# One stream for all 16 pairs of expert and batch, and ScalarE normalising the first batch in the joint norms

## The chip, the cores and the metric

The kernel runs on one core of one Trainium2 chip. The metric is the device time of one execution in microseconds; several executions are made and their median is compared. A trace of one profiled execution gives the rows below.

## The reference, cut to what matters

Two layers, each a mixer followed by a feed-forward part, on x of 2 batches x 1024 tokens x 128 features, with a layer norm ahead of each of the four parts (A: gated linear scan and a SiLU network; B: six blocks of windowed attention and GELU network; C: linear attention; D: mixture of experts) and a norm with a residual addition behind each. The two pieces that the change touches:

```python
def norm(x):                       # layer norm; the rms form leaves the mean out
    return (x - mean(x)) / sqrt(var(x) + 1e-5)

# part D: 8 experts choose 128 tokens each, per batch
affinity = softmax(norm(x) @ gate_w)                  # [B, S, 8]
for b in range(2):
    for e in range(8):
        places = the 128 tokens of batch b with the highest affinity to e
        h = norm(x)[b, places]                        # gather, 128 x 128
        h = silu(h @ Wg[e]) * (h @ Wu[e]) * affinity[b, places, e]
        y[b, places] += h @ Wd[e]                     # scatter
x = x + norm(y)
```

## The kernel before

Tokens lie 128 to a tile, NT = 8 tiles a batch, B = 2 batches; S = 1024, HALF = 512 columns is one PSUM bank (PS is 8 banks). Features lie on the partitions in the feature-major layout. Each engine's program is written by hand in blocks; a block ends in a barrier of all engines. Within a block semaphores called flows order the engines: one engine's instruction increments a flow, another's waits for the next count.

`norm(*parts)` (L209) is called ten times in source; nine calls are joint, with one part for each batch, and the tenth, inside the loop of part D, has a single part and runs twice. Its VectorE program (L232) makes statistics of every part in halves of four tiles (bn_stats L239, bn_aggr L242, variance plus epsilon L253, in the rms form L247 and L250), then normalises every tile of every part in `normalise` (L255), one tile an instruction (L261 in the rms form, L265 otherwise), into NTOK, then adds the residual, if there is one, with one instruction a part (L278). GpSimd raises the variance to the power -0.5 for each half (L288). PE transposes normalised tiles (L226) where the part has a destination in feature-major layout, and ScalarE copies each half from PSUM to the destination (L298). A source in feature-major layout is transposed to tokens first (L218). Of the nine joint calls four have a token source and a destination (L330, L518, L1129, L1478), two are rms with a feature source and a destination (L331, L388), three have a feature source and a residual (L459, L1060, L1402). The final norm (L1750) reads tokens from PSUM and has a residual.

Part D: after the lists of places are made, a hardware loop runs over the batches (L1605). In it a block copies the normalised tokens and affinities to TOK (L1631 ScalarE, L1635 VectorE) and clears a zero tile, the next block runs the experts, and the norm follows. `step(n, i)` handles expert n and prepares expert n + 1 (n + 2 on VectorE); `run` executes steps -2 and -1, a hardware loop of three iterations of two steps, and the last two. In a step PE does in this order: gather of expert n + 1 with a one-hot matrix (L1645, 8 matmuls), transposes of the hidden tile HD of expert n (L1652), broadcast of the places of expert n + 1 to all partitions, two banks, each one matmul (L1660), transpose of the chosen tokens (L1665), down projection (L1670), gate and up projection of n + 1 (L1676), scatter with the transposed one-hot matrix into banks 6 and 7 (L1682, 8 matmuls). Ahead and behind, L1688 and L1692 open and close the accumulation of those banks with a zero product. A float32 matmul counts as two instructions in the trace, a transpose as one. ScalarE makes the sigmoid (L1701) and copies out of PSUM (L1705 chosen, L1709 hidden transposed HTD, L1712, L1716). VectorE multiplies (L1724, L1727), compares the broadcast places with its own partition's place for the transposed one-hot (L1733, 1024 columns), and makes the one-hot of expert n + 2 (L1740). There is one one-hot buffer and one transposed one.

## Time and profile before

| | |
|---|---|
| median of 3 runs | 2147.94 us (2147.43 to 2148.8) |
| the profiled execution, its time | 2145.2 us |
| its span | 2143.4 us |
| PE busy | 1921.5 us, 90% of the span |
| VectorE busy | 1709.2 us, 80% |
| ScalarE busy | 1400.0 us, 65% |
| GpSimd busy | 1245.5 us, 58% |
| chain that ended last | VectorE lines of the last norm, 0% each |
| stages on the trace's axis | A to 113.4, B to 1802, C to 1940, D to the end; part B's own program from 124 to 1785 |

In the rows below DVE is VectorE, ACT ScalarE, POOL GpSimd, PEld PE's weight load. A row of a timeline has the start, the time from the first start to the last end, the engine, the line, the operation, output and inputs, the shape and the count; in brackets stands the idle time of the engine before it and what ended it. The profile's names leave out numbers at the end: COSL in part D is the one-hot pair of buffers, QKT and XB the tokens, SQ the sigmoid, R and RR the hidden tiles.

### The profile page before, as it was taken

The numbers are of one execution on the slowest core, as the hardware profiler recorded it, in microseconds if no ns is written. First come the engines' busy times: TensorE is split into PE (matmuls) and PEld (weight loads), VectorE is DVE, ScalarE is ACT, GpSimd is POOL, SyncE is SP. The second block draws the span as 40 slices with busy tenths as digits, with TensorE's granted clock in tenths as the row PEclk, the third lists the DMA queues.
The fourth block names the chain that finished last, engine by engine and source line by source line (L and its number), as shares of the span: only waits on it lengthen the run. The fifth ranks groups of instructions, "written<-read, shape, count | busy, mean of one in ns | idle before, by whom it ended". The sixth has DMA issues, their size and how long they took to land. (4 is left out here: it accounts for less than half of the span.)

```text
span 2143.4 us, 79777 instructions
## 1 busy us (share of the span) xinstructions
PE 1921.5 (90%) x33524; PEld 1454.4 (68%) x33524; DVE 1709.2 (80%) x3962; ACT 1400.0 (65%) x5039; POOL 1245.5 (58%) x871
## 2 busy tenths in 40 slices
PE   4769999999999999999999999999999984491677
PEld 2348778687786886868868688687786862251455
DVE  5689889698796996979969789698896965787544
ACT  3159779597695985968959689597795961340222
POOL 2258768388584885857858668586683841031000
PEclk8879999999999999999999999999999997795799
DMA  3011112021120211212112121021110100001000
GB/s 113 0 42 42 31 50 58 21 78 35 44 59 22 76 39 36 58 29 73 41 35 57 33 69 44 24 63 40 51 52 17 42 26 13 0 2 60 1 1 20
DMA packets 88224, 85.65 MB, mean 40 GB/s; under 512 B 15392, under 2 KB 83008, under 8 KB 87232
## 3 DMA queue, kind: packets, MB, share of 16 engines
q1 hardware_dynamic: 87872, 80.63, 13.5%
q8 instruction: 260, 4.26, 0.8%
q14 instruction: 92, 0.75, 0.1%
HBM read 25.51 MB, written 1.05 MB: 12 GB/s over the span
## 5 line engine op out<-in xcount | busy, mean ns | idle before, releaser
L1050 POOL TENSOR_TENSOR RN<-N,minus_half 128x8 f32<-128x8 f32 x384 | 632.5, 1647 | 169.3 <-DVE N L978 169.3
L888 ACT ACTIVATE PB<-PS,NMX 128x64 f32<-128x64 f32 x1536 | 469.5, 334 | 30.3 <-DVE NMX L998 30.2
L647 PE MATMUL PS<-WQ,XS 128*128 128x256 f32 x1536 | 434.6, 406 | 7.5 <-SPq L591 5.9
L888 ACT ACTIVATION_READ_ACCUMULATOR PB<-PS,NMX 128x1 f32 x1536 | 344.7, 224 | 0.0
L647 PEld LDWEIGHTS PS<-WQ,XS 128*128 128x128 f32 x1536 | 261.3, 190 | 44.5 <-SPq L591 6.1
L1045 POOL TENSOR_TENSOR RR<-R 128x512 f32<-128x512 f32 x192 | 244.4, 1273 | 78.1 <-DVE QK L1008 78.1
L871 ACT ACTIVATE QKT<-PS 128x512 f32<-128x512 f32 x384 | 229.0, 596 | 87.3 <-PE PS L733 87.2
L1045 POOL TENSOR_TENSOR RR<-R1B,R2B 128x512 f32<-128x512 f32 x192 | 245.0, 1276 | 69.4 <-DVE QK L1008 69.4
L1008 DVE SCALAR_TENSOR_TENSOR QK<-RN,RR 128x512 f32<-128x512 f32 x384 | 261.7, 681 | 0.6 <-POOL RR L1045 0.6
L978 DVE TENSOR_REDUCE N<-SQ 128x8 f32<-128x512 f32 x384 | 259.5, 676 | 0.0
L854 ACT ACTIVATE SQ<-PS 128x512 f32<-128x512 f32 x384 | 237.1, 617 | 8.0 <-PE PS L647 7.7
L754 PE MATMUL PS<-WQ,XS 128*128 128x128 f32 x1536 | 234.2, 275 | 0.0
L733 PE MATMUL PS<-ident,QK 128*128 128x128 f32 x1536 | 230.8, 273 | 2.4 <-DVE QK L1008 2.1
L879 ACT ACTIVATE XB<-PS 128x512 f32<-128x512 f32 (+1 forms) x386 | 232.8, 603 | 0.1
L288 POOL TENSOR_TENSOR rstd<-ve,minus_half 128x4 f32<-128x4 f32 x40 | 40.4, 1010 | 320.0 <-DVE ve L253 292.1
L733 PEld LDWEIGHTS PS<-ident,QK 128*128 128x128 f32 x1536 | 191.7, 141 | 47.2 <-issue 6.2
L794 PE MATMUL PS<-XB,VS 64*64 64x32 f32 x6144 | 212.1, 224 | 2.0 <-ACT BIG L860 1.8
L794 PE MATMUL PS<-XB 64*64 64x32 f32 x6144 | 204.4, 219 | 1.1 <-issue 1.1
L754 PEld LDWEIGHTS PS<-WQ,XS 128*128 128x128 f32 x1536 | 201.7, 192 | 0.0
L794 PEld LDWEIGHTS PS<-XB,VS 64*64 64x64 f32 x6144 | 162.0, 133 | 37.3 <-ACT BIG L860 1.8
L998 DVE TENSOR_REDUCE NMX<-PS 128x4 f32<-128x256 f32 x384 | 163.0, 424 | 22.1 <-PE PS L778 6.1
L778 PE MATMUL PS<-QKT 64*32 64x64 f32 x12288 | 174.5, 222 | 0.3 <-ACT QKT L871 0.2
(263 smaller groups left out, 3506.2 us busy)
## 6 DMA issues: line engine op xcount, KB each, us to landing
VS<-XB SPq DMA_DIRECT2D x384, 96.0 KB, 2.1
VS<-XB SPq DMA_DIRECT2D x288, 32.0 KB, 1.9
WQ<-in_wqkv SPq DMA_DIRECT2D x40, 192.0 KB, 2.6
WO<-in_wo SPq DMA_DIRECT2D x6, 512.0 KB, 4.2
XS<-XT SPq DMA_DIRECT2D x10, 256.0 KB, 3.5
XS<-XT SPq DMA_DIRECT2D x10, 255.8 KB, 4.2
BIG<-in_wgu SPq DMA_DIRECT2D x1, 2048.0 KB, 8.1
W<-in_w SPq DMA_DIRECT2D x6, 341.0 KB, 3.3
```

What stands on the lines that cost most here:

```text
L647: mm = nc.tensor.matmul(PQ[:, m % 2, j * 256:(j + 1) * 256], XSb[b][:, t0:t0 + P], WQ[:, pair * 384:pair * 384 + 256], start=True, stop=True)
L733: tr = nc.tensor.transpose(TQ[:, (2 * k + j) * P:(2 * k + j + 1) * P], QK[:, g % 2, j, k, :], ident[:, :])
L754: last = nc.tensor.matmul(PX[:, j * P:(j + 1) * P], XSb[b][:, t0:t0 + P], WQ[:, pair * 384 + 256:(pair + 1) * 384], start=True, stop=True)
L794: mm = nc.tensor.matmul(PO[DH * h:DH * h + DH, t, WIN * w:WIN * w + WIN], vals[keys, c, w // 2, DH * h:DH * h + DH], XB[keys, (g - 1) % CH ...
L854: nc.scalar.activation(SQ[:, m % 2, :, :].rearrange("p g d -> p (g d)"), PQ[:, m % 2, :], ACT.Square).then_inc(sq_in.sem, 1)
L871: nc.scalar.activation(QKT[:, :, WIN + c * CB * P:WIN + (c + 1) * CB * P], TQ.rearrange("p (k s) -> p k s", k=2), ACT.Copy).then_inc(qkt_i ...
L879: nc.scalar.activation(XB[:, g % CH, cols], PX[:, cols], ACT.Copy)\
L888: ex = nc.scalar.activation(PB[:, g % 2, u, :], SC[:, h, DH * t:DH * t + DH], ACT.Exp, bias=NMX[:, u:u + 1], accum_out=PSUMS[:, g % 2, u:u ...
L978: nc.vector.tensor_reduce(N2[:, g % 2, :], SQ[:, g % 2, :, :], AX.X, ALU.add)\
L1008: nc.vector.scalar_tensor_tensor(QKg[(g + 1) % 2], RN[:, (g + 1) % 2, :].unsqueeze(2) .to_broadcast([P, 8, DH]), 1e12, RRg, ALU.min, ALU.m ...
L1045: nc.gpsimd.tensor_tensor(RR[:, :, :], R1k[(g + 1) % 2][:, :, :], R2k[(g + 1) % 2][:, :, :], ALU.add)\
L1050: nc.gpsimd.tensor_tensor(RN[:, g % 2, :], N2[:, g % 2, :], minus_half[:, :], ALU.pow)
```

## The change

In the norms with more than one part, ScalarE normalises part 0 (Identity with scale 1/std and bias -mean/std; Copy with a scale in the rms form), and VectorE only part 1. VectorE makes the bias of part 0 with one more instruction after the third half of the statistics. GpSimd signals part 0's powers on a flow of their own.

In part D the two batches are one stream of RUNS = 16 steps, written out without hardware loops, expert n // 2 of batch n % 2. TOK, the one-hot and its transposed form have two buffers each. The scatter of batch 0 goes to banks 4 and 5, that of batch 1 to 6 and 7. The places are broadcast one half at a time into one bank, `places(n, h)`: the first half of expert n at the end of step n - 1, the second in step n. The final norm is one joint call.

```diff
         def norm(*parts, rms=False, eps=1e-5):
+            split = len(parts) > 1
...
                         if part.dst is not None:
+                            ready = ntok_first if split and k == 0 else ntok_in
                             for t in range(NT):
-                                pe.wait_ge(ntok_in.sem, ntok_in.take())
+                                pe.wait_ge(ready.sem, ready.take())
...
                             statistics(k, part, range(4 * h, 4 * h + 4))
+                            if split and not rms and (k, h) == (1, 0):
+                                dve.wait_ge(rstd_first.sem, rstd_first.take(NH))
+                                nc.vector.scalar_tensor_tensor(nmr[:, :], mvk[0][:, :, 0], -1.0, rstdk[0][:, :],
+                                                               ALU.mult, ALU.mult).then_inc(shift_first.sem, 1)
                     for k, part in enumerate(parts):
-                        for h in range(NH):
-                            normalise(k, part, range(4 * h, 4 * h + 4))
+                        if not split or k > 0:
+                            for h in range(NH):
+                                normalise(k, part, range(4 * h, 4 * h + 4))
...
                 @block.scalar
                 def _(act):
+                    if split:
+                        for t in range(NT):
+                            if rms:
+                                if t % 4 == 0:
+                                    act.wait_ge(rstd_first.sem, rstd_first.take())
+                                nc.scalar.activation(NTOKk[0][:, t, :], parts[0].source(0, t), ACT.Copy,
+                                                     scale=rstdk[0][:, t:t + 1]).then_inc(ntok_first.sem, 1)
+                            else:
+                                if t == 0:
+                                    act.wait_ge(shift_first.sem, shift_first.take())
+                                nc.scalar.activation(NTOKk[0][:, t, :], parts[0].source(0, t), ACT.Identity,
+                                                     scale=rstdk[0][:, t:t + 1], bias=nmr[:, t:t + 1])\
+                                    .then_inc(ntok_first.sem, 1)
...
+                    def places(n, h):
+                        row = 32 * h + n % B * NE + n // B
+                        nc.tensor.matmul(PS[:, 0, :], identb[0:HR, row:row + 1].to_broadcast([HR, P]),
+                                         RKB[:, :], start=True, stop=True)\
+                            .then_inc(place_ps.sem, 1)
...
+                            pe.wait_ge(hott_in.sem, hott_in.take())
+                            places(n, 1)
...
+                        if now:
+                            pe.wait_ge(hott_in.sem, hott_in.take())
+                        if coming:
+                            places(n + 1, 0)
...
+                    for k in range(4):
+                        nc.tensor.matmul(PS[:, 4 + k, :], ident[:, :], YT[:, 0:HALF], start=True, stop=False)
+                    for n in range(-2, RUNS):
+                        step(n)
+                    for k in range(4):
+                        nc.tensor.matmul(PS[:, 4 + k, :], ident[:, :], YT[:, 0:HALF], start=False, stop=True)
...
+                    def transposed(n, h):
+                        dve.wait_ge(place_ps.sem, place_ps.take())
+                        nc.vector.tensor_scalar(ONEHOT_Tk[n % 2][:, h * HALF:(h + 1) * HALF], PS[:, 0, :], PLACE,
+                                                None, ALU.is_equal).then_inc(hott_in.sem, 1)
...
+                            if n > 1:
                                 dve.wait_ge(hott_used.sem, hott_used.take())
...
+                            transposed(n, 0)
+                        m = n + 2
+                        if m < RUNS:
+                            if m > 1:
+                                dve.wait_ge(hot_used.sem, hot_used.take())
...
+                        if 0 <= n:
+                            transposed(n, 1)
...
-                norm(Part(tokens=lambda t: bank_tiles(6, t), residual=x_batch(b)))
+            norm(*[Part(tokens=lambda t, b=b: bank_tiles(4 + 2 * b, t), residual=x_batch(b)) for b in range(B)])
```

PE in a step of the expert stream, before: L1645 gather, L1652 transposes of HD, L1660 broadcasts, L1665 transpose of the chosen, L1670 down, L1676 up, L1682 scatter.

```order
L1645 MATMUL PS<-QKT,COSL 128x136 x8
L1652 MATMUL PS<-ident,R 128x128 x2
L1660 ISA
L1660 MATMUL PS<-RKB,identb 128x512
L1660 ISA
L1660 MATMUL PS<-RKB,identb 128x512
L1665 MATMUL PS<-ident,SINL 128x128
L1670 MATMUL PS<-BIG,RR 128x128 x2
L1676 MATMUL PS<-BIG,SINL 128x512
L1682 MATMUL PS<-R,COSL 128x128 x8
```

The same of the changed kernel, with the waits: L1663 gather, L1669 transposes of HD, L1654 broadcast of one half, L1676 transpose of the chosen, L1682 down, L1689 up, L1698 scatter.

```order
L1663 MATMUL PS<-XB,COSL 128x136 [waits one_hot_ready]
L1663 MATMUL PS<-XB,COSL 128x136 x7
L1669 MATMUL PS<-ident,R 128x128 [waits hidden_tile_ready]
L1669 MATMUL PS<-ident,R 128x128
L1654 MATMUL PS<-RKB,identb 128x512 [waits one_hot_transposed_ready]
L1676 MATMUL PS<-ident,SINL 128x128 [waits chosen_tokens_ready]
L1682 MATMUL PS<-BIG,RR 128x128 [waits hidden_feature_major]
L1682 MATMUL PS<-BIG,RR 128x128
L1689 MATMUL PS<-BIG,SINL 128x512 [waits chosen_tokens_feature_major]
L1654 MATMUL PS<-RKB,identb 128x512 [waits one_hot_transposed_ready]
L1698 MATMUL PS<-R,COSL 128x128 [waits expert_output_ready]
L1698 MATMUL PS<-R,COSL 128x128 x7
```

One of the two broadcasts moved from ahead of the transpose of the chosen to behind the up projection, and each now waits for VectorE's comparison of the half before it.

VectorE at the same place, before (L1733 is the comparison of 1024 columns, L1740 the one-hot):

```order
L1724 TENSOR_TENSOR R<-PS,SQ 128x256 [waits sigmoid_ready]
L1727 ISA [waits silu_ready]
L1727 SCALAR_TENSOR_TENSOR R<-PS,SINL,R 128x256
L1733 TENSOR_SCALAR COSL<-PS,SINL 128x1024 [waits places_broadcast,expert_output_scattered]
L1740 ISA [waits one_hot_used]
L1740 TENSOR_TENSOR COSL<-SINL,BIG 128x1024
```

and now (L1744 compares one half, L1764 is the one-hot):

```order
L1751 TENSOR_TENSOR R<-PS,SQ 128x256 [waits sigmoid_ready]
L1753 SCALAR_TENSOR_TENSOR R<-PS,SINL,R 128x256 [waits silu_ready]
L1744 TENSOR_SCALAR COSL<-PS,SINL 128x512 [waits places_broadcast,expert_output_scattered]
L1764 TENSOR_TENSOR COSL<-SINL,BIG 128x1024 [waits one_hot_used]
L1744 TENSOR_SCALAR COSL<-PS,SINL 128x512 [waits places_broadcast]
```

The comparison is two, with the one-hot between them, and the address instructions (ISA) of the loop are gone.

ScalarE in the first two norms of the changed kernel (L322 and L317 normalise part 0, L330 is the copy from PSUM that was L298):

```order
L322 ACTIVATE NTOK<-X,nmr,rstd 128x128 [waits shift_of_first_part_ready]
L322 ACTIVATE NTOK<-X,nmr,rstd 128x128 x7
L330 ACTIVATE XS<-PS 128x512 [waits normalised_half_in_psum] x4
L216 UNCONDITIONAL_BRANCH
L310 UNCONDITIONAL_BRANCH [waits barrier_Pool_Activation_PE_DVE_SP_release]
L317 ACTIVATE NTOK<-PS,rstd 128x128 [waits rstd_of_first_part_ready]
L317 ACTIVATE NTOK<-PS,rstd 128x128 x3
L317 ACTIVATE NTOK<-PS,rstd 128x128 [waits rstd_of_first_part_ready]
L317 ACTIVATE NTOK<-PS,rstd 128x128 x3
```

Before, ScalarE's program there held the four copies L298 alone; the eight tiles stand ahead of them, with no table load between.

## Rows read from the trace of the kernel before

**Rows 1.** Timeline, first norm (token source), VectorE and ScalarE.

```profile
14.55 0.17 DVE L253 TENSOR_SCALAR ve<-mv 128x4 f32<-128x4 f32 x1
...
15.89 4.19 DVE L265 TENSOR_SCALAR NTOK<-X,mv,rstd 128x128 f32<-128x128 f32 x16
...
20.64 0.60 ACT L298 ACTIVATE XS<-PS 128x512 f32<-128x512 f32 x1 [0.43 <-PE PS L226]
```

**Rows 2.** Timeline, second norm (rms), with PE's transposes ahead of it.

```profile
21.50 1.73 PEld L218 LDWEIGHTS PS<-ident,XS 128*128 128x128 f32 x16 [1.19 <-issue]
...
23.84 1.01 POOL L288 TENSOR_TENSOR rstd<-ve,minus_half 128x4 f32<-128x4 f32 x1 [6.75 <-DVE ve L250]
...
28.11 4.22 DVE L261 TENSOR_SCALAR NTOK<-PS,rstd 128x128 f32<-128x128 f32 x16
...
28.27 1.01 POOL L288 TENSOR_TENSOR rstd<-ve,minus_half 128x4 f32<-128x4 f32 x1 [0.47 <-POOLq L62]
...
32.90 0.69 ACT L298 ACTIVATE XT<-PS,BIG 128x512 f32<-128x512 f32 x1 [0.35 <-PE PS L226]
```

**Rows 3.** Timeline, fourth norm (residual), VectorE's normalising and additions.

```profile
105.95 5.19 DVE L265 TENSOR_SCALAR NTOK<-PS,mv,rstd 128x128 f32<-128x128 f32 x16
...
111.06 2.35 DVE L278 TENSOR_TENSOR X<-X,NTOK 128x1024 f32<-128x1024 f32 x2
```

**Rows 4.** Timeline, PE in one steady step of the expert stream.

```profile
2044.70 0.38 PE L1652 MATMUL PS<-ident,R 128*128 128x128 f32 x2
...
2045.02 0.60 PE L1660 MATMUL PS<-RKB,identb 48*128 48x512 bf16 x2
...
2045.72 0.69 PE L1670 MATMUL PS<-BIG,RR 128*128 x4
...
2046.34 1.12 PE L1676 MATMUL PS<-BIG,SINL 128*128 x2
...
2047.30 1.95 PE L1682 MATMUL PS<-R,COSL 128*128 128x128 f32 x16
...
2049.09 2.02 PE L1645 MATMUL PS<-QKT,COSL 128*128 128x136 f32 x16
...
2050.94 0.38 PE L1652 MATMUL PS<-ident,R 128*128 128x128 f32 x2
```

**Rows 5.** Timeline, ScalarE and VectorE in the same step.

```profile
2045.17 0.38 ACT L1709 ACTIVATE RR<-PS 128x256 f32<-128x256 f32 x1
...
2047.92 0.42 DVE L1724 TENSOR_TENSOR R<-PS,SQ 128x256 f32<-128x256 f32 x1 [1.53 <-ACT SQ L1701]
...
2048.38 0.48 DVE L1727 SCALAR_TENSOR_TENSOR R<-PS,SINL,R 128x256 f32<-128x256 f32 x1
...
2049.29 1.28 DVE L1733 TENSOR_SCALAR COSL<-PS,SINL 128x1024 f32<-128x1024 f32 x1 [0.43 <-PE PS L1682]
```

**Rows 6.** Timeline, first statistics of both final norms; first normalising of the second.

```profile
2061.92 0.89 DVE L239 BATCH_NORM_STATS2 bn<-PS 128x6 f32<-128x128 f32 x4 [5.20 <-PEq L1637]
...
2130.92 0.89 DVE L239 BATCH_NORM_STATS2 bn<-PS 128x6 f32<-128x128 f32 x4 [5.20 <-PEq L1637]
...
2133.48 2.64 DVE L265 TENSOR_SCALAR NTOK<-PS,mv,rstd 128x128 f32<-128x128 f32 x8
```

**Rows 7.** Timeline, ScalarE in part C, 128x128 with a scale pointer.

```profile
1863.79 2.45 ACT L1370 ACTIVATE BIG<-SINL,BIG 128x128 f32<-128x128 f32 x8 [14.57 <-PEq L1131]
```

**Rows 8.** Timeline, start of the expert stream and PE's first wait.

```profile
1999.13 1.28 ACT L1631 ACT_TABLE_LOAD   x1 [38.44 <-PEq L1524]
...
2001.78 3.75 PE L1688 MATMUL PS<-YT,ident 128*128 128x512 f32 x4 [3.55 <-PEq L1628]
...
2005.32 2.95 PE L1645 MATMUL PS<-QKT,COSL 128*128 128x136 f32 x16
...
2013.82 0.60 PE L1660 MATMUL PS<-RKB,identb 48*128 48x512 bf16 x2 [0.93 <-DVE COSL L1733]
```

**Rows 9.** Windows: stretch, length, busy (count) by engine, granted clock, DMA share, GB/s.

```profile
2006.70:2007.70 1.00, 1.00 (x8) 1.00 (x8) 0.00 (x0) 0.00 (x0) 0.00 (x0) 0.74 0.00 0
```

More of the change, by code:

```diff
@@ L94, in mixed_layers_kernel @@
         rstd, rstd1 = sb("rstd", [P, NT]), sb("rstd1", [P, NT])
+        nmr = sb("nmr", [P, NT])
         NTOKk, bnk, mvk = (NTOK, NTOK1), (bn, bn1), (mv, mv1)
@@ L197, in mixed_layers_kernel @@
         res_in = flow("normalised_tile_for_residual")
+        rstd_first = flow("rstd_of_first_part_ready")
+        shift_first = flow("shift_of_first_part_ready")
+        ntok_first = flow("normalised_tile_of_first_part_ready")
         class Part:
@@ L230, in _ @@
                     ntok_in.settle(pe)
+                    if split and parts[0].dst is not None:
+                        ntok_first.settle(pe)
                 @block.vector
@@ L271, in _ @@
                             statistics(k, part, range(4 * h, 4 * h + 4))
+                            if split and not rms and (k, h) == (1, 0):
+                                dve.wait_ge(rstd_first.sem, rstd_first.take(NH))
+                                nc.vector.scalar_tensor_tensor(nmr[:, :], mvk[0][:, :, 0], -1.0, rstdk[0][:, :],
+                                                               ALU.mult, ALU.mult).then_inc(shift_first.sem, 1)
                     for k, part in enumerate(parts):
-                        for h in range(NH):
-                            normalise(k, part, range(4 * h, 4 * h + 4))
+                        if not split or k > 0:
+                            for h in range(NH):
+                                normalise(k, part, range(4 * h, 4 * h + 4))
                     for k, part in enumerate(parts):
                         if part.residual is not None:
-                            dve.wait_ge(res_in.sem, res_in.take(NT))
+                            ready = ntok_first if split and k == 0 else res_in
+                            dve.wait_ge(ready.sem, ready.take(NT))
                             nc.vector.tensor_tensor(part.residual, part.residual, NTOKk[k][:, :, :], ALU.add)
@@ L280, in _ @@
                         f.settle(dve)
+                    if split and not rms:
+                        rstd_first.settle(dve)
+                    if split and parts[0].residual is not None:
+                        ntok_first.settle(dve)
                 @block.gpsimd
@@ L284, in _ @@
                     for k in range(len(parts)):
+                        done = rstd_first if split and k == 0 else rstd_in
                         for h in range(NH):
@@ L288, in _ @@
                             nc.gpsimd.tensor_tensor(rstdk[k][:, cols], vek[k][:, cols], minus_half[:, 0:4],
-                                                    ALU.pow).then_inc(rstd_in.sem, 1)
+                                                    ALU.pow).then_inc(done.sem, 1)
                     var_in.settle(pool)
@@ L293, in _ @@
                 def _(act):
+                    if split:
[11 more added lines that the diff above has]
+                                    .then_inc(ntok_first.sem, 1)
+                        (rstd_first if rms else shift_first).settle(act)
                     for k, part in enumerate(parts):
@@ new lines, in mixed_layers_kernel, with _ @@
+            TOKk = [r[:, 0:NT * (D + NE)].rearrange("p (t n) -> p t n", n=D + NE)
+                    for r in (QKT[:, :, :].rearrange("p k s -> p (k s)"), XB[:, :, :].rearrange("p c n -> p (c n)"))]
+            ONEHOTk = [r[:, 0:4, :].rearrange("p a (c n) -> p (a c) n", n=P) for r in (COSL, COSL1)]
+            ONEHOT_Tk = [r[:, 4:8, :].rearrange("p a b -> p (a b)") for r in (COSL, COSL1)]
+            RUNS = B * NE
+            with nc.Block() as block:
+                @block.scalar
+                def _(act):
+                    for b in range(B):
+                        nc.scalar.activation(TOKk[b][:, :, 0:D], XTOK[:, b * NT:(b + 1) * NT, :], ACT.Copy)
+                @block.vector
+                def _(dve):
+                    for b in range(B):
+                        nc.vector.tensor_copy(TOKk[b][:, :, D:D + NE], AF[:, :, b * NE:(b + 1) * NE])
+                    nc.vector.memset(YT[:, 0:HALF], 0.0)
```

228 lines of the change are left out of this document (90 added, 138 removed).

## The prediction

> **What bounds the kernel now.** The page's chain of waits names only VectorE lines of the last norm, each at 0%, so it ranks nothing; I went stage by stage with the timeline. Stage B, from about 124 to 1785 us, keeps its code, so whatever is won lies in the ten norms and in the expert stream after 1999 us.
>
> A norm is one serial run of VectorE: statistics of four halves, then 16 tiles normalised. With a feature-major output, PE and ScalarE follow tile by tile and are through 0.6 to 1.1 us after VectorE: 4.19 us of normalising from 15.89, last copy of ScalarE from 20.64 to 21.24 [rows 1]; in the rms form 4.22 us from 28.11, last copy to 33.59 [rows 2]. With a residual it is VectorE alone: 5.19 us of normalising from PSUM, then two additions, 2.35 us [rows 3]. ScalarE is idle meanwhile.
>
> In the expert stream PE is the bound. The reader is to see that each PE row starts where the one before it stops being issued: scatter 1.79 us (2047.30 to 2049.09), then the gather; the transposes of HD 0.32 for two; the two place broadcasts and the one transpose of the chosen 0.70 together, so 0.54 and 0.16; down 0.62, up 0.96. From HD's transposes at 2044.70 to the next at 2050.94 it is 6.24 us [rows 4]. ScalarE and VectorE have slack inside it [rows 5]. But each batch fills and drains this pipeline anew and ends in its own norm: the first statistics of the two final norms are 2130.92 - 2061.92 = 69.00 us apart, and 8 steps of 6.24 are 49.9 [rows 6]. So 19.1 us a batch are fill, drain, barriers and norm.
>
> **Norms, ScalarE takes batch 0.** A ScalarE activation with one pointer operand costs 0.09 us more than one without: 0.69 against 0.60 for 128x512 [rows 1, 2]. Eight of 128x128 with a scale pointer take 2.45 us, some 0.295 each [rows 7]. For scale and bias no row of this size stands; the ends are 0.295 (the second pointer hidden) and 0.48 (the pointers not overlapped at all). I take 0.295 + 0.09 = 0.39, nearest to the row.
>
> *Three residual norms.* VectorE adds one small instruction (the shift, 0.17 as the ve row of [rows 1]) and drops eight tiles. It is then 0.17 + 2.6 to the additions in place of 111.06 - 105.95 = 5.11 [rows 3]: 2.34 saved. ScalarE starts about 1.05 us before the statistics end and needs 8 x 0.39 + 0.1 = 3.2, so it is done 2.15 after their end, before VectorE's 2.8: covered. If it took 0.48 a tile it would end at 2.9, costing nothing much. 3 x 2.34 = 7.0 (bounds 5 to 8).
>
> *Two rms norms.* ScalarE needs no shift and can begin when the first rstd is there, 23.84 + 1.01 = 24.85, and is through batch 0 before the statistics end at 28.11. VectorE then has batch 1: four tiles to 29.15, and the last four wait for GpSimd's fourth pow, 28.27 + 1.01 = 29.28, so they end at 30.4. One transpose (0.25) and one copy (0.69) later it is 31.5 against 33.59: 2.05 each, 4.1 (3 to 5) [rows 2].
>
> *Four norms with a token source.* ScalarE gets its shift at 14.72 + 0.17, starts at 14.95 and ends at 18.1; VectorE ends at 18.35 with the pow wait. PE, in order, takes batch 0's last tile at 18.3 and only then batch 1's eight: 0.11 each at full clock (1.73 for 16), twice that at half [rows 2]. ScalarE's copies are queued behind all its eight tiles, so its last ends at 20.2 to 21.0 against 21.24 [rows 1]. I take 1.0 for the first norm, which ran at full clock, and about 0.5 for the others: 2.6 (0 to 5).
>
> Here a rule speaks against the change. The trace prices a tile at 0.39 on ScalarE (my estimate) against 4.19/16 = 0.26 on VectorE [rows 1]. The Trainium skill, "ScalarE: Activation LUTs", rules for kernel authors, gives add and multiply to VectorE. By the row the division still pays where both work at once; by the rule it would not, and the norm terms would go to about nothing. That is the first rival below.
>
> Norms: 7.0 + 4.1 + 2.6 = 13.7.
>
> **The stream, 16 pairs in one.** It removes one fill, drain and norm: +19.1 [rows 6]. Against it:
>
> - The step. PE's order changes: only one broadcast (0.27) now lies between HD's transposes and the transpose of the chosen. Count from the start of HD's transposes, 2044.70. HTD is copied by 2045.17 + 0.38 [rows 5], that is at 0.85, visible at 0.9; PE would now want it at 0.32 + 0.27 + 0.16 = 0.75. So down starts at 0.9 where it could at 0.75: 0.15 a step, 16 x 0.15 = 2.4 (ends 0 and 0.4 a step). The second broadcast moves behind up and takes what it took. Its condition is VectorE's second half. VectorE starts its step 1.58 after up (2047.92 against 2046.34), takes about 1.0 for its two products (0.42 and 0.48 with the wait between), 0.65 for the first half of the comparison (half of 1.28) and as much as a whole comparison, 1.28, for the one-hot of as many columns [rows 4, 5]: it is free some 6.0 after HD's transposes of the step before began, in a step of 6.39. The second half runs from 0.75 to 1.4, wanted at 2.5. Covered by 1.1 us; first half covered by 1.9.
> - The start. PE zeroes four banks: eight matmuls in place of four. Before, they went at 0.86 each and the first gather took 2.95 and ended at 2008.27, 6.5 after the first of them began [rows 8]; the clock was 0.50 until about 2007.2, the 0.74 of that slice being half of it at each level [rows 9]. Now: 5.45 us at half clock (6.4 matmuls), 1.6 at 0.43, gather 1.86 and its pipelined end 0.1, together 8.1: -1.6.
> - A second copy of tokens ahead of PE's start: load, copy and barrier were 2001.78 - 1999.13 = 2.65, of which the load was 1.28, so a copy is some 1.0: -1.0. The load goes from there (the build has none): +1.3 [rows 8].
> - The end: four more closing matmuls at 0.43, -1.7.
> - The joint final norm: two more halves of statistics 2.56, the shift 0.17, one more addition 1.17; the normalising stays at 2.64: -3.9 [rows 3, 6].
> - PE's wait in the first step (idle 0.93 before 2013.82, for the whole one-hot of 1024 columns) shrinks to about 0.2: +0.7 [rows 8]. A batch's last step has the same wait, and no broadcast of a next expert to pay for with it: as much again, less the 0.27 of the second half, +0.5.
>
> 19.1 - 2.4 - 1.6 - 1.0 + 1.3 - 1.7 - 3.9 + 0.7 + 0.5 = 11.0 (8 to 14). With the loops the 0.1 us branches and register reads go too, but PE shows no gap at them, so nothing is counted.
>
> **Sum.** 13.7 + 11.0 = 24.7. The profiled execution has a span of 2143.4 and a time of 2145.2; 2145.2 - 24.7 = 2120.5. The median of the three runs, 2147.94, is 2.7 above it, so the forecast for a median is 2123.2, call it 2123.
>
> **Rivals.**
>
> *ScalarE's half ends last.* If its tiles take near 0.5 beside VectorE, or PE's clock falls to half in the shorter norms, then batch 1's transposes and the copies queue behind ScalarE. Token norms give 0, the rms norms 1 each, the residual ones 1 each: 5 in place of 13.7, time about 2132. For: the token norms are already within 1 us of it. Against: in the rms and residual forms ScalarE starts over 1 us before VectorE. 15%.
>
> *More than forecast.* The token norms give 1.5 each, HTD comes in time, and PE reaches full clock earlier in the stages behind the norms (the first projection after the second norm ran at half clock): 4 + 2.4 + 2 more, some 33 saved, 2115. 14%.
>
> *Slower.* PE waits twice in every step for a half of the comparison. The mechanism is in the trace: in the first step PE stood 0.93 us for that comparison [rows 8]. Two such waits in 16 steps are 16 x 1.86 = 29.8, so 5 us slower, 2153. It needs VectorE to be later than worked out above by 1.1 + 0.9 us a step, or the first half to be late by 1.9 + 0.9. It decides from 1.7 us a step. Against: VectorE's step adds up to under 5 of 6.39 us. 3%.
>
> *Nothing left.* The same wait at 1.6 us a step, or a stage B that starts or ends in another phase, eats the gain: within 4.3 us of 2148. 3%.
>
> **How the numbers follow.** Forecast 65%, its own range 2117 to 2129; the four rivals 15, 14, 3 and 3. A range of 2115 to 2132 takes in the bounds of the costs (16 to 32 saved) and leaves out some 20%. 0.2% is 4.3 us, about what a measurement of this kernel can tell from no change. Faster 0.94, same 0.03, slower 0.03.
>
> **What would show it.** Right: the starts of PE's HD transposes 6.3 to 6.5 us apart over 16 steps, with 0.1 to 0.2 us of PE's idle time before down and ended by ScalarE; ScalarE's Identity tiles 0.39 apart and finished before VectorE's in the residual norms; the gap from the first statistics to the residual addition 2.3 shorter in those; the final statistics once, near 2102 on the new axis. Wrong: steps over 6.6; PE waiting for the transposed one-hot; Identity tiles of 0.45 and more; a table load in a norm. What would upset the forecast most is PE's clock, which no row of before can foretell for the new order.

## The result, and the profile after

| | before | after |
|---|---|---|
| median | 2147.68 us (2147.35 to 2148.8, 4 runs) | 2125.76 us (2124.28 to 2127.85, 4 runs) |
| the profiled execution, its time | 2145.2 | 2125.36 |
| its span | 2143.4 | 2123.6 |
| PE, VectorE, ScalarE busy | 1921.5, 1709.2, 1400.0 | 1930.0, 1688.3, 1421.5 |

The ratio of the times is 0.9898, 95% interval 0.9881 to 0.9915: 21.9 us faster by the medians, 19.8 by the two profiled spans. The forecast was 2123, range 2115 to 2132, for 24.7 us saved.

The timeline of after, first the fourth norm (residual), rows that answer to [rows 3]. VectorE's statistics, shift, eight tiles and two additions; ScalarE's eight tiles:

```profile
96.87 0.89 DVE L246 BATCH_NORM_STATS2 bn<-PS 128x6 f32<-128x128 f32 x4 [0.98 <-PE PS L222]
...
100.70 0.16 DVE L281 SCALAR_TENSOR_TENSOR nmr<-mv,rstd 128x8 f32<-128x8 f32 x1
...
102.06 2.64 DVE L272 TENSOR_SCALAR NTOK<-PS,mv,rstd 128x128 f32<-128x128 f32 x8
104.60 2.36 DVE L291 TENSOR_TENSOR X<-X,NTOK 128x1024 f32<-128x1024 f32 x2
```

```profile
100.90 2.91 ACT L322 ACTIVATE NTOK<-PS,nmr,rstd 128x128 f32<-128x128 f32 x8 [10.15 <-DVE nmr L281]
```

From normalising to the additions it is 2.54 us where it was 5.11, and ScalarE ends at 103.81, 0.9 before VectorE's last tile. The second norm (rms), which answers to [rows 2]:

```profile
22.30 0.89 DVE L246 BATCH_NORM_STATS2 bn<-PS 128x6 f32<-128x128 f32 x4 [3.99 <-PE PS L222]
...
24.99 1.14 ACT L317 ACTIVATE NTOK<-PS,rstd 128x128 f32<-128x128 f32 x4 [4.10 <-POOL rstd L306]
...
28.21 2.33 DVE L268 TENSOR_SCALAR NTOK<-PS,rstd 128x128 f32<-128x128 f32 x8
...
31.12 0.69 ACT L330 ACTIVATE XT<-PS,BIG 128x512 f32<-128x512 f32 x1 [0.53 <-PE PS L231]
```

The first norm (token source), which answers to [rows 1]. VectorE is done at 18.31, but PE's last transposes, nine weight loads from 18.07 to 19.85, take 0.2 us each, and the last copy ends at 20.89:

```profile
14.82 3.19 ACT L322 ACTIVATE NTOK<-X,nmr,rstd 128x128 f32<-128x128 f32 x8 [4.73 <-DVE nmr L281]
...
15.96 2.35 DVE L272 TENSOR_SCALAR NTOK<-X,mv,rstd 128x128 f32<-128x128 f32 x8
...
18.07 1.78 PEld L231 LDWEIGHTS PS<-ident,NTOK 128*128 128x128 f32 x9 [0.20 <-ACT NTOK L322]
...
20.29 0.60 ACT L330 ACTIVATE XS<-PS 128x512 f32<-128x512 f32 x1 [0.26 <-PE PS L231]
```

PE in one steady step of the stream, which answers to [rows 4]: up, first half of the broadcast, scatter, gather, transposes of HD, second half, chosen, down, up.

```profile
2044.46 1.02 PE L1689 MATMUL PS<-BIG,SINL 128*128 128x512 f32 x2
2045.42 0.39 PE L1654 MATMUL PS<-RKB,identb 48*128 48x512 bf16 x1
2045.73 2.05 PE L1698 MATMUL PS<-R,COSL 128*128 128x128 f32 x16
2047.62 2.02 PE L1663 MATMUL PS<-QKT,COSL 128*128 128x136 f32 x16
2049.48 0.38 PE L1669 MATMUL PS<-ident,R 128*128 128x128 f32 x2
2049.79 0.39 PE L1654 MATMUL PS<-RKB,identb 48*128 48x512 bf16 x1
2050.11 0.33 PE L1676 MATMUL PS<-ident,SINL 128*128 128x128 f32 x1
2050.38 0.71 PE L1682 MATMUL PS<-BIG,RR 128*128 128x128 f32 x4
2050.93 1.02 PE L1689 MATMUL PS<-BIG,SINL 128*128 128x512 f32 x2
```

Up starts 6.47 us after up. Down starts 0.90 after HD's transposes, where before it was 1.02.

The start of the stream and the final norm, which answer to [rows 6, 8]:

```profile
1992.51 5.35 PE L1704 MATMUL PS<-YT,ident 128*128 128x512 f32 x8 [3.39 <-PEq L1638]
1997.69 2.02 PE L1663 MATMUL PS<-QKT,COSL 128*128 128x136 f32 x16
...
2103.54 3.60 PE L1708 MATMUL PS<-YT,ident 128*128 128x512 f32 x8
...
2107.43 0.89 DVE L246 BATCH_NORM_STATS2 bn<-PS 128x6 f32<-128x128 f32 x4 [6.29 <-PEq L1649]
```

The span cut at the first statistics of the ten norms, in us (each entry is a difference of two starts of such rows, as 107.26 - 96.87 = 10.39 for the fourth norm). "After" was profiled twice; A2 and A3 are the rms norms, A4, B2, C2 and the final one the residual ones, the other four have a token source:

| stretch | before | after | after again | saved | forecast |
|---|---|---|---|---|---|
| A1 token norm, to A2 | 11.35 | 11.44 | 10.98 | -0.1 | 1.0 |
| A2 rms norm, gates and scan | 30.49 | 28.82 | 29.57 | 1.7 | 2.05 |
| A3 rms norm, SiLU network | 48.15 | 45.75 | 46.01 | 2.4 | 2.05 |
| A4 residual norm | 12.87 | 10.39 | 10.38 | 2.5 | 2.34 |
| B1 token norm and stage B | 1675.81 | 1676.86 | 1675.44 | -1.1 | 0.5 |
| B2 residual norm, to C1 | 18.12 | 15.72 | 15.71 | 2.4 | 2.34 |
| C1 token norm, linear attention | 120.12 | 119.95 | 121.15 | 0.2 | 0.5 |
| C2 residual norm, to D1 | 16.09 | 13.66 | 13.64 | 2.4 | 2.34 |
| D1 token norm, part D, to the end | 199.55 | 190.15 | 190.37 | 9.4 | 11.5 |

So the residual and the rms terms came nearly whole, and what is missing stands in the rows with a token norm. Not all of that is the change's: A1, B1 and C1 differ between the two profiles of the changed kernel by 0.5, 1.4 and 1.2.

### The profile page after: what moved, and what is told of

Same layout as the page of the kernel before. It is cut to its first block and busy times, and to the rows that moved or that the text cites. A ratio compares the mean times of both kernels' runs of the same rounds, so it can differ in the third digit from the quotient of the medians.

```text
span 2123.6 us, 79458 instructions
## 1 busy us (share of the span) xinstructions
PE 1930.0 (91%) x33524; PEld 1456.1 (69%) x33524; DVE 1688.3 (80%) x3905; ACT 1421.5 (67%) x5112; POOL 1246.3 (59%) x871
```

## The experiments

Gains are the difference of the medians of a kernel and of the kernel before in the same rounds, the intervals those of the ratio. The changed kernel itself, measured in two sets of rounds, gave 21.9 and 20.1 us. The kernel before had 2147.68 in the first of these sets and 2143.84 to 2145.69 in all later ones, so the 20.1 is the better measure beside the gains below.

**Norms alone.** The kernel before with the changed `norm`, its part D left as it was.

> The kernel before with one part of the change alone: ScalarE normalises batch 0 in the nine joint norms; part D keeps its two passes over eight experts and its single norms. By the sum on record the norms give 13.7 us (7.0 in the residual norms, 4.1 in the rms ones, 2.6 in those with a token source). By the trace of the changed kernel they give 7.3 + 3.8 + 1.1 = 12.2 in themselves, and some 2 to 3 us are lost again behind them where PE runs at half clock, so 9 to 10 us here. The rival that ScalarE's half ends last gives 5.

Measured: 2136.65 against 2145.69, 9.0 us, ratio 0.9954 (0.9938 to 0.9971). The sum on record, 13.7, lies just outside the interval (6.2 to 13.3 us), the trace's account within it. The residual norms show the same 10.38, 15.66 and 13.71 as in the changed kernel.

**Stream alone.**

```diff
-            split = len(parts) > 1
+            split = False
```

> The changed kernel with VectorE normalising all tiles in every norm, so that only the stream of 16 and the joint final norm are left of the change. By the sum on record the stream gives 11.0 with a split final norm; without the split that norm takes 5.1 for its 16 tiles in place of 2.8, so 8.7 remain. The trace of the changed kernel says 10.7 - 2.3 = 8.4. If norms and stream are independent, the gain of this kernel and that of the norms alone, plus 2.3, add up to the 21.9 of both. If the stream had been helped by the split norms ahead of it, this kernel gains under 6.

Measured: 2138.52, 7.2 us, 0.9964 (0.9949 to 0.9978). With the 2.3 for the final norm the two parts sum to 18.5 beside 21.9 and 20.1: they are independent as far as these runs can tell. The interval of the 7.2, 4.7 to 10.9 us, does not exclude the 6 below which the split norms would have helped the stream. The trace speaks against such help: from the first statistics of D1 to those of the final norm it is 173.44 us here and 173.98 in the changed kernel.

**Token norms given back.**

```diff
-            split = len(parts) > 1
+            split = len(parts) > 1 and (rms or parts[0].dst is None)
```

> The changed kernel, but in the four norms with a token source and a feature-major destination VectorE normalises both batches again. By the sum on record this costs 2.6 us against the changed kernel. By its trace those norms gained 0.35 + 0.22 + 0.36 + 0.21 = 1.1 and the stages behind them lost up to 2.5 by PE's half clock, so this kernel is between 1.1 slower and 1.4 faster: no difference that this many rounds tell.

Measured: 2125.18, 20.5 us, 0.9901 (0.9885 to 0.9918), the same as the changed kernel. In four norms the change brought nothing that the time shows. Where their 1.1 us went can be read ahead of the stream. PE's gate products of part D (L1513) in the changed kernel, then in this one:

```profile
1943.77 3.55 PE L1513 MATMUL PS<-BIG,XN 128*128 128x8 f32 x16 [0.93 <-PEq L216]
1947.18 3.56 PE L1513 MATMUL PS<-BIG,YT 128*128 128x8 f32 x16
```

```profile
1945.20 1.92 PE L1513 MATMUL PS<-BIG,XN 128*128 128x8 f32 x16 [0.93 <-PEq L216]
1946.98 3.14 PE L1513 MATMUL PS<-BIG,YT 128*128 128x8 f32 x16
```

The windows say why (stretch, length, busy time and count of PE, PEld, DVE, ACT and POOL, granted clock, DMA share, GB/s), the changed kernel first:

```profile
1942.00:1944.00 2.00, 1.07 (x6) 0.70 (x5) 0.00 (x0) 1.44 (x3) 0.00 (x0) 0.50 0.00 0
1944.00:1946.00 2.00, 2.00 (x11) 2.00 (x11) 0.00 (x0) 1.76 (x2) 0.00 (x0) 0.50 0.00 0
```

```profile
1944.00:1946.00 2.00, 1.07 (x10) 0.91 (x9) 0.00 (x0) 1.42 (x2) 0.00 (x0) 0.99 0.00 0
1946.00:1948.00 2.00, 2.00 (x18) 2.00 (x18) 0.22 (x1) 1.18 (x2) 0.00 (x0) 0.86 0.00 0
```

With VectorE alone the clock had risen to 0.99 when the products began; with the shorter norm it stood at 0.50, 1.2 GHz, throughout. The kernel before had 1.00 there too, and took 2.06 us for the first sixteen. This is the one place where the clock went with the norm in every profile, as the table in the next section has it: 1.92 to 2.12 us in the three kernels in which VectorE normalises all tiles there, 3.55 in the six in which ScalarE takes eight.

**PE kept busy.** Ahead of the work behind a norm, matmuls that nobody reads:

```diff
+        def warm(bank, times):
+            for _ in range(times):
+                nc.tensor.matmul(PS[:, bank, :], identb[:, :], identb[:, :].unsqueeze(1).to_broadcast([P, 4, P]),
+                                 start=True, stop=True)
...
+                    if parts[0].dst is not None:
+                        warm(2, 10 if parts[0].features is None else 6)
```

> The changed kernel with added matmuls whose results nobody reads: 10 of 128x512 bf16 ahead of the transposes in the norms with a token source, 6 in the rms norms, 8 and 3 ahead of stage B's first projection, 4 and 6 ahead of the expert stream. They lie in idle time of PE. If the half clock of PE behind the norms is what ate the token norms' gain, the clock is at 1.00 there, the 16 transposes of a norm take half as long, stage B and the stream start at full clock: 3 us faster than the changed kernel (2 to 5). If ScalarE's eight tiles and the copies queued behind them set the end, as the rival on record has it, the norms keep their length and only the starts of stage B and of the stream gain, 1 to 1.5 us. If the added matmuls delay the first transposes, it is slower.

Measured: 2118.28 against 2145.69, 27.4 us, 0.9865 (0.9849 to 0.9882), some 6 more than the changed kernel. PE in the token norm of stage B:

```profile
106.53 4.43 PE L215 MATMUL PS<-identb 128*128 128x512 bf16 x10 [9.12 <-PEq L221]
111.04 3.89 PE L238 MATMUL PS<-ident,NTOK 128*128 128x128 f32 x16
```

```profile
110.00:112.00 2.00, 1.86 (x6) 0.51 (x4) 1.93 (x16) 1.51 (x4) 1.43 (x3) 0.69 0.01 4
112.00:114.00 2.00, 1.72 (x7) 0.83 (x7) 1.86 (x7) 2.00 (x6) 0.83 (x1) 1.00 0.00 0
```

From the first statistics to ScalarE's last copy this norm took 10.26 us before, 10.04 in the changed kernel, 9.14 here; A1 10.39, 10.03, 9.15; C1 10.38, 10.03, 9.15; D1, where the clock rose and fell again, stayed at 10.03. So about 0.9 us of each of these three token norms had gone to PE's half clock, and the forecast's 1.0 for the first was a full-clock figure. With the 0.9 of the norm in it, stage B's stretch is 1673.64 and the linear attention's 118.11, shorter by 1.8 to 3.2 and by 1.8 to 3.0 than in the two profiles of the changed kernel. The stream did not gain (174.06 us from the first statistics of D1 to those of the final norm, against 173.98): the expected gain there did not come. Zero products and first gather took 5.5 us in place of 7.2, but the first zero product started 60.8 us behind the statistics of D1 and not 59.1: ahead of the stream the added matmuls were not all in idle time.

**Half for ScalarE, and zero products of one pass.**

```diff
+            half = split and not rms and parts[0].dst is not None
+            mine = 4 if half else NT
...
-                        nc.tensor.matmul(PS[:, 4 + k, :], ident[:, :], YT[:, 0:HALF], start=True, stop=False)
+                        nc.tensor.matmul(PS[:, 4 + k, :], identb[:, :], ZERO, start=True, stop=False)
```

with tiles `mine` to 7 of batch 0 normalised by VectorE, and ZERO a bf16 tile of zeros read as 512 columns.

> The changed kernel with two edits in different places, each read at its own place of the trace. (1) In the four norms with a token source ScalarE normalises only tiles 0 to 3 of batch 0, VectorE tiles 4 to 7 and batch 1. If ScalarE's eight tiles, with PE's transposes and ScalarE's copies queued behind them, set the end of these norms, each gets 0.5 to 1 us shorter; if PE's half clock over 16 transposes sets it, each stays within 0.3. (2) The zero products that open and close the four banks of the expert stream are bf16 with one pass of 512 columns in place of float32 with two: at the measured 0.43 a pass at full clock and half of that for bf16, the closing takes 0.9 in place of 3.4 us, 2.6 less. The opening loses 4.1 us of its own length, but then PE works less at the start and the rise of the clock may come as late as before: 0 to 3 less there. Together 4 to 7 us faster than the changed kernel. If the closing products lay beside other work, (2) gives under 1.

Measured: 2115.0 against 2145.49, 30.5 us, 0.9855 (0.9839 to 0.9872): 8.6 to 10.4 more than the changed kernel, above what was expected. (1): the token norms take 9.43, 9.44, 9.44 and 9.49 where they took 10.03: 0.6 each. ScalarE's eight tiles do set part of the end. VectorE, now with twelve tiles, is done 8.27 us behind the first statistics and no longer 7.46, so the end is VectorE's. (2): the opening is

```profile
1987.45 1.86 PE L1710 MATMUL PS<-bandmask,identb 128*128 128x512 bf16 x4 [3.01 <-PEq L1644]
...
1989.11 2.83 PE L1669 MATMUL PS<-QKT,COSL 128*128 128x136 f32 x16
```

From the first zero product to the end of the first gather 4.5 us in place of 7.2, from the first closing one to the statistics 1.3 in place of 3.9: 5.3 together. From D1 to the final norm it is 165.62 us in place of 173.98, 8.4 less; of the other 3.1 the gate products of D are 1.6, which ran at 1.00 here (1.92 us for the first sixteen), and the norm 0.5.

**Without the second half of the broadcast,** the one behind HD's transposes.

```diff
-                            pe.wait_ge(hott_in.sem, hott_in.take())
-                            places(n, 1)
...
-                        if 0 <= n:
-                            transposed(n, 1)
```

> The changed kernel without the second half of every pair's place broadcast, the matmul behind the transposes of HD, and without its comparison on VectorE; the second half of the transposed one-hot is left out of the computation, so the scatter reads old values there. If the down projection starts at 0.9 because ScalarE's copy of HD's transposes is late, as the sum on record says, the broadcast lies in time that PE would otherwise wait: the step stays at 6.4 to 6.5 and the time within 1.5 us of the changed kernel. If PE's own work sets the step, it is 0.32 shorter, 16 x 0.32 = 5.1 us. If VectorE's comparisons were what PE waits for, the gain is over 6.

Measured: 2125.13, 20.4 us, 0.9903 (0.9887 to 0.992), and from D1 to the final norm 173.98, the same to the hundredth. PE from HD's transposes to up:

```profile
2048.70 0.38 PE L1669 MATMUL PS<-ident,R 128*128 128x128 f32 x2
2049.33 0.33 PE L1674 MATMUL PS<-ident,SINL 128*128 128x128 f32 x1 [0.25 <-ACT SINL L1720]
2049.61 0.71 PE L1680 MATMUL PS<-BIG,RR 128*128 128x128 f32 x4
```

and ScalarE's copy of HD's transposes:

```profile
2049.18 0.38 ACT L1724 ACTIVATE RR<-PS 128x256 f32<-128x256 f32 x1
```

Down still starts 0.91 after HD's transposes; PE waits for ScalarE instead. The broadcast in that place is free, as the sum had it. The long wait, 0.25, is ahead of the transpose of the chosen tokens, for their copy. Behind it down starts 0.28 later, where before it was 0.16 (the prediction's reading of [rows 4]), and ScalarE's copy of HD's transposes ends at 2049.56, 0.05 ahead of down. That fits the 0.9 of the sum, which had down wait for that copy.

**Without the first half,** the one behind up.

```diff
-                        if coming:
-                            places(n + 1, 0)
...
-                            transposed(n, 0)
```

> The changed kernel without the first half of every pair's place broadcast, the matmul behind the gate and up projection, and without its comparison; the first half of the transposed one-hot is left out of the computation. The scatter then follows the projection at once. By every account in which PE bounds the end of the step, the step is 0.32 shorter, 16 x 0.32 = 5.1 us (4 to 6) faster than the changed kernel, unless the scatter then waits for ScalarE's copy of the down projection, which ends 0.8 us before that matmul now: it does not.

Measured: 2117.97, 27.5 us, 0.9866 (0.985 to 0.9883). The stretch from D1 to the final norm is 165.74, 8.2 less, and up starts every 5.95 us: 0.52 a step, not 0.32. PE's weight loads behind up (L1689 or L1688) show what it was made of, the changed kernel first:

```profile
2044.35 0.30 PEld L1689 LDWEIGHTS PS<-BIG,SINL 128*128 128x128 f32 x2
2045.41 0.09 PEld L1654 LDWEIGHTS PS<-RKB,identb 48*128 48x128 bf16 x1 [0.76 <-issue]
2045.73 1.86 PEld L1698 LDWEIGHTS PS<-R,COSL 128*128 128x128 f32 x16 [0.23 <-issue]
```

```profile
2048.22 0.30 PEld L1688 LDWEIGHTS PS<-BIG,SINL 128*128 128x128 f32 x2
2048.92 2.02 PEld L1695 LDWEIGHTS PS<-R,COSL 128*128 128x128 f32 x16 [0.40 <-issue]
```

The small load starts 1.06 after up's; the scatter's load, where it follows at once, 0.70. The broadcast costs that 0.36 ahead of it and its own 0.32, less 0.16 that the scatter's issue is shorter behind it (1.78 against 1.94). VectorE's comparison was left out with it, but VectorE does not bound the step, as the next kernel shows.

**VectorE made later** by four comparisons a step that nobody reads.

> The changed kernel with four more comparisons of 512 columns on VectorE ahead of the first half of every step's, with results that nobody reads: 4 x 0.65 = 2.6 us a step. The sum on record gave VectorE 1.9 us of slack for the first half and 1.1 for the second: PE would then wait 1.5 a step at least, 24 us slower. The trace of the changed kernel shows VectorE idle for 1.54 before the second half and done 1.3 before the scatter wants it, 2.8 together: then 0.3 to 0.5 a step, 5 to 8 us slower. No difference at all would mean that VectorE never bounds here.

Measured: 2137.43 against 2145.49, 8.1 us faster than before (0.996, 0.9946 to 0.9975) and so 12 to 14 slower than the changed kernel. HD's transposes stand 6.88 apart (2047.70, 2054.58, 2061.47), 0.42 more: 6.7 over 16 steps, as the trace's reading had it, and far from the 1.5 a step of the sum. The stretch grew by 11.7: 2.3 in the first pair, in which PE stands 2.25 for VectorE and the HD transposes are 8.77 apart, 5.6 in the fourteen that follow, and 3.7 behind the last HD transposes, where it stands 2.23 for VectorE and the last scatter takes 3.36 us. In a steady step PE waits ahead of the broadcast of the second half, for the comparison of the first:

```profile
2055.34 0.39 PE L1655 MATMUL PS<-RKB,identb 48*128 48x512 bf16 x1 [0.37 <-DVE COSL L1747]
```

So VectorE has 2.6 - 0.42 = 2.2 us of slack in a step, where the slower rival decided at 1.7.

**The first half moved** behind the scatter.

```diff
-                        if coming:
-                            places(n + 1, 0)
...
                             mm.then_inc(hott_used.sem, 1)
+                        if coming:
+                            places(n + 1, 0)
```

> The kernel with ScalarE's half and bf16 zero products, and with the first half of the next pair's place broadcast moved from ahead of the scatter to behind it, VectorE making the one-hot of two pairs on before it compares the first half. Leaving that half out shortened the step by 0.52 us, not by the 0.27 that a broadcast takes beside another one. If those 0.25 are the handing over from the wide projection to a load of 48 rows, between scatter and gather it costs 0.3 and the step falls from 6.47 to 6.25, 3.5 us over 16 steps. If any lone broadcast costs it, the step stays at 6.47. If VectorE is late with its second comparison after the swap, PE waits ahead of the scatter and it is slower.

Measured: 2116.38 against 2143.84, 27.5 us, 0.9868 (0.9851 to 0.9884), no gain over the kernel that it was made from (30.5). From D1 to the final norm it is 169.13 us against 165.62 there: 1.6 are the gate products, here at half clock again with the same norm (3.55), 0.8 the first pair. The step is 6.46:

```profile
2047.63 0.09 PEld L1660 LDWEIGHTS PS<-RKB,identb 48*128 48x128 bf16 x1
...
2047.95 1.92 PEld L1669 LDWEIGHTS PS<-XB,COSL 128*128 128x128 f32 x16 [0.23 <-issue]
```

Behind the scatter a lone broadcast costs the same 0.52 of the step, so it is not the handing over from the wide projection alone.

**Both gains together, and less of the added matmuls.** All added matmuls, with 22 more in the linear attention, on top of the half and the bf16 zero products:

> The kernel with ScalarE taking half of batch 0 in the token norms and with bf16 zero products, and with the added matmuls that keep PE busy: 12 in a token norm ahead of the transposes and one behind each of the first four tiles, 6 in the rms norms, 8 and 3 ahead of stage B, 22 while PE waits in the linear attention, 4 and 6 ahead of the expert stream. The added matmuls alone won some 6 us, the half and the zero products alone some 9 (both against the changed kernel through the kernel before). The token norms are the one place where both act: 10.03 us from the first statistics to the last copy went to 9.15 and to 9.44; together 8.7 to 8.9 is expected. The opening of the stream is the second: with full clock at once and bf16 products. Sum: 12 to 16 us faster than the changed kernel, 34 to 38 faster than the kernel before. If the two gains are the same idle time, no more than 9 to 10.

Measured: 2112.68 against 2143.84, 31.2 us, 0.9849 (0.9832 to 0.9865). Less than the expected 34 to 38: the token norms take 9.29, 9.29, 9.29 and 9.48, not 8.8, and the stretch from D1 to the final norm is 166.69 against 165.62 without the added ones. In the token norms VectorE's twelve tiles, done 8.27 us behind the first statistics in every kernel with the half (8.46 in D1), leave the clock only the 1.0 behind them to shorten. In the stream the first zero product started 58.4 us behind the statistics of D1 and not 56.3, and the opening won only half of that back.

> The kernel with ScalarE's half, bf16 zero products and added matmuls, with fewer of them: 9 in a token norm in place of 12, which had put off PE's first transpose from 4.51 to 4.83 us behind the first statistics, and none ahead of the expert stream. If these delays ate the sum of the two gains, the token norms go from 9.29 to 8.8 to 9.0 us, the stream is as long as with the bf16 products alone (165.6 from the first statistics ahead of part D to those of the final norm), and the kernel is 2 to 3 us faster than the one with all added matmuls, some 34 faster than the kernel before. If the gains are the same idle time, it stays at 31.

Measured: 2111.47 (2108.2 to 2114.14) against 2145.61, 34.1 us, 0.9837 (0.9823 to 0.9851), and 14.1 us below the changed kernel in the same rounds. The stream's stretch is 165.54 as expected; the token norms stayed at 9.29 (9.48 in D1), though PE's first transpose came at 4.51 again: its delay was not what held them, VectorE's end at 8.27 was. This beats both kernels. How much of its lead over the 31.2 is real the intervals don't tell.

> The changed kernel itself, on the chip and in the rounds of the version above, as the measure for all comparisons with it: 21 to 22 us faster than the kernel before, as in its first runs. Its first executions lay 3.6 us apart; if that is the moment at which PE's clock rises behind the norms, its profile here shows other lengths than the first one in the stages that begin at half clock (stage B, the linear attention, part D) by 1 to 3 us each, and the same within 0.1 in the norms.

Measured: 2125.56 against 2145.61, 20.1 us, 0.9902 (0.9887 to 0.9917). Its stretches stand in the table as "after again": the residual norms repeat to 0.02, stage B and the linear attention differ by 1.4 and 1.2, as expected, while part D, from which 1 to 3 us were expected too, repeats to 0.2. Nor does stage B's 1.4 lie at its start, which repeats to 0.3 us. The largest difference lies near its end: from the statistics near 1630 to those near 1755 it is 126.58 us in the first profile, where the clock had 0.62 from 1739 to 1748, and 123.95 in this one, where it stayed at 1.00. The kernel before had 0.66 from 1747 to 1752, and 125.52.

## Why the prediction was right

The gain of 24.7 was forecast too high by a tenth to a fifth: 2.8 us by the medians of the first rounds, 4.6 by those of the second, 4.9 by the spans. The smallest of the three owes something to luck, since the kernel before was at 2147.68 in those rounds and at 2143.84 to 2145.69 in all later ones. The first statistics of the final norm stood at 2107.43, not near 2102.

*Residual norms, 7.0: right, measured 7.3* (2.5 + 2.4 + 2.4). ScalarE's tile from PSUM is 2.91 / 8 = 0.36, from SBUF 0.39, the estimate. It ended ahead of VectorE, as worked out. The Trainium skill's rule ("ScalarE: Activation LUTs", rules for kernel authors) that gives add and multiply to VectorE did not decide: a tile is dearer on ScalarE, 0.39 against 0.26, and the norms alone still won 9.0 us, since both engines work at once.

*Rms norms, 4.1: right, 3.8.* From the first statistics to the last copy 33.59 - 22.20 = 11.39 became 9.51, 1.88 in place of 2.05. (The prediction's "through 0.6 to 1.1 us after VectorE" is short by these rows: to the end of the last copy it is 1.16 and 1.26. The sums use the ends and are not touched.)

*Token norms, 2.6: the step that failed.* 0.36 + 0.22 + 0.35 + 0.21 = 1.1 by the rows, and nothing that the time shows. The term took the first norm at full clock, because the transposes of [rows 2] behind it ran so; but inside it PE works in single tiles, each weight load takes 0.18, and batch 1's eight transposes come in a row behind ScalarE's last tile at 0.21 each, where 0.11 was counted. The range of this term reached to 0. The two causes were both in the text (tiles queued behind ScalarE's eight, PE's clock), and the runs part them: 0.6 for the first alone, 0.9 for the second alone, 0.74 for both together (10.03 - 9.29), since then VectorE ends last.

*PE's clock behind the norms: named as what no row foretells, and counted at nothing.* Three places show what it can cost, and only one of them goes with the change. The table has the sixteen transposes ahead of the second norm, the stretch from the first statistics of B1 to the next norm in stage B, and the first sixteen gate products of D, in us:

| kernel | tiles of the token norms | transposes | start of B | gate products |
|---|---|---|---|---|
| before | VectorE | 1.73 | 146.79 | 2.06 |
| stream alone | VectorE | 3.27 | 148.44 | 2.12 |
| token norms given back | VectorE | 3.27 | 147.08 | 1.92 |
| changed | eight on ScalarE | 3.27 | 147.99 | 3.55 |
| changed, again | eight on ScalarE | 1.73 | 148.24 | 3.55 |
| norms alone | eight on ScalarE | 3.27 | 146.54 | 3.55 |
| without the second half | eight on ScalarE | 3.27 | 147.08 | 3.55 |
| without the first half | eight on ScalarE | 3.27 | 148.19 | 3.55 |
| VectorE made later | eight on ScalarE | 1.73 | 147.91 | 3.55 |

The gate products lost 1.5 us by the change (with four tiles on ScalarE they came out both ways, 1.92 in one kernel and 3.55 in another). The transposes and the start of stage B are long or short with either norm, and the changed kernel itself has both lengths of the transposes. Windows of stage B's start, before and after; the first projection began at 129.28 before and at 123.15 after:

```profile
130.00:132.00 2.00, 2.00 (x7) 1.55 (x6) 0.00 (x0) 0.60 (x1) 0.00 (x0) 0.50 0.69 264
132.00:134.00 2.00, 1.10 (x4) 0.39 (x2) 1.98 (x4) 0.60 (x1) 0.62 (x1) 0.68 0.27 104
```

```profile
128.00:130.00 2.00, 2.00 (x5) 1.39 (x6) 1.56 (x3) 0.06 (x1) 2.00 (x2) 0.50 0.00 0
130.00:132.00 2.00, 2.00 (x7) 1.53 (x7) 1.85 (x4) 0.53 (x1) 2.00 (x3) 0.50 0.00 0
132.00:134.00 2.00, 1.87 (x43) 1.57 (x42) 0.93 (x3) 1.50 (x4) 2.00 (x2) 0.95 0.00 0
```

Before, PE was at full clock some 4 us after its first matmul; after, it needed 9. Of the other kernels with the same norms, the norms alone needed 4 (0.79 in the window from 126 and 1.00 from 128, from a first matmul near 123). So what A1 and B1 lack in the table of stretches is not a price of the change that these runs show: it moves between executions.

The whole account: the norms gave 7.3 + 3.8 + 1.1 and the stream 10.7, together 22.9; the gate products took 1.5 back; the other 1.6 up to the 19.8 of the spans lie in A1, A2, A3, B1 and C1, which vary by about as much from profile to profile.

*Stream, 11.0: right in sum.* By the rows it is the 9.4 of the last stretch less 0.2 of the token norm, plus the 1.5 of the gate products: 10.7. (The same sum gives 11.4 with the token norms given back.) The step was mis-sized: 6.39 forecast, 6.47 measured, 1.3 us over 16 steps. Down began at 0.9 as forecast, and leaving the second half out changed nothing; but the first half behind up was taken at 0.27 and costs 0.52. That it came out only 0.08 dearer is since other pieces got shorter: down to up 0.55 in place of 0.62, and up to scatter, where no broadcast lies between, 0.86 in place of the 0.96 of [rows 4]; what shortened them is not shown. The start gained more than forecast, by luck: zeroing and first gather took 7.2 in place of 8.1, as the clock rose 3.4 us after the first zero product, where before it was 5.4; in the changed kernel's second profile it was 3.9 and 7.5, in the stream alone 5.8 and 8.4.

*The slower rival* needed VectorE to be late by 1.7 a step. It is not: 2.2 of slack were measured, more than the 1.1 and 1.9 of the sum. Nor did ScalarE's half end last in the residual and rms norms; in the token norms it did, which was that rival's condition in a part of its place.

## What to carry to other kernels

When two engines share a serial stretch, the gain is what the slower of the followers leaves: look who takes the tiles, in what order, and at which clock, before half the work is counted as saved. A stretch of work that becomes shorter can cost TensorE its clock in what follows, as in part D here; but the clock also moves from execution to execution, so read it in several profiles of both kernels before a loss is put down to the change. A lone small matmul between large ones is priced by leaving it out, not by the pitch of two in a row.

## What the runs showed of the hardware that was not expected

- A broadcast of 512 bf16 columns with a 48-row stationary costs 0.27 next to another one ([rows 4]) and 0.52 a step alone behind the wide projection; behind the scatter the step came out the same. Why is open. Behind HD's transposes it costs nothing, since PE would wait.
- TensorE's clock fell within a norm, behind single transposes spaced by ScalarE's tiles: in D1 the kernel with the added matmuls had 0.87, 0.99 and then 0.50 in the three windows of 2 us from 1930, with PE busy for 1.44, 1.48 and 2.00 of them.
- At 20 to 24 us the clock column says 1.00 for the changed kernel while its transposes take 0.2 each, as elsewhere at 0.50. There the durations decide.
